# A four-layer graph network on one core: moving a product's scaling from VectorE to ScalarE and GpSimd in the first layer

## The chip, the cores and the metric

The program runs on one core of a Trainium2 chip. The metric is the device time of one execution in microseconds (us). Beside it stands the profile of one execution: its span is the time between the first and the last instruction that the profiler recorded. TensorE is PE in the profile (PEld is its weight load), VectorE is DVE, ScalarE is ACT, GpSimd is POOL and SyncE is SP.

## The reference, cut to what matters

Sixteen inputs `x` of 512 nodes by 128 features pass through four layers, each followed by a residual sum and a layer norm. The change is in the first layer alone, and in one step of the preparation of the second:

```python
def _conv(x, adj):
    return x * jnp.sum(adj, axis=1)[None, :, None]
adaptive = softmax(relu(node_vec1 @ node_vec2), axis=1)
outputs = [x]
for adj in (support0, support1, adaptive):     # both supports are adj here
    x1 = _conv(x, adj);  outputs.append(x1)
    x1 = _conv(x1, adj); outputs.append(x1)
out = concatenate(outputs, axis=2) @ W + b
x = _layernorm(x + out)
...
A_hat = A_norm * dinv[:, None] * dinv[None, :]  # second layer, dinv = rsqrt(deg)
```

`_conv` only scales a node's row by a number. So the layer is a sum of five products of `x` with 128x128 weights, `x @ (W0+I) + s*(x @ Wa) + s^2*(x @ Wb) + a*(x @ Wc) + a^2*(x @ Wd) + b`, with `s` and `a` one number for each node (`coef[:, 0..3, t]`).

## The kernel before

The first stage (`phase_a`) treats the sixteen inputs in eight pairs, and software-pipelines three things over ten slots: slot q has the first layer of pair q (`now`), the aggregation with the 512x512 `A_hat` for pair q-1 (`one`) and the hidden product of pair q-2 (`two`). Each engine has its own instruction queue, written out by hand in `slot(q, ...)`, and executes it strictly in order; semaphores tie the queues together.

A pair has four node tiles t = 0..3 of 128 nodes (both inputs of the pair side by side, so 128x256 elements). For each tile:

- TensorE, `products(q, t)`: the five products into three PSUM banks; even and odd tiles have banks of their own, so `products(q, t)` waits until tile t-2 has been mixed (`mixed`). `products(q, 0)` also waits for the high and low parts of `x` (`xt_hi`, `xt_lo`).
- ScalarE, `scale_first(q, t)` (L467): `mix = coef0 * product 1`.
- VectorE, `combine(q, t)`: three chained multiply-adds (L658), one for each of products 2, 3 and 4, then the plain product 0 (L660).
- GpSimd, `add_bias(q, t)` (L324): adds the bias row. After it VectorE takes the statistics (`count_mix`, L673); after tile 3 they become `rstd` (GpSimd computes the power, L110) and `shift` (L683, `shift_of`).
- In the next slot ScalarE normalizes (`norm`, L478), rounds to the high part (`split_x1`, L486), GpSimd subtracts for the low part (`split_x1`, L329), and TensorE aggregates (L141 to L143, `psum<-shared`).

The order of the queues in a slot of the middle (q = 2 to 6) is, with the other input's work written as i = 0, 1:

- GpSimd: bias of tile 0, `split_x1` 0, bias of tile 1, `split_x1` 1 (L329), bias of tile 2, `split_x` 0 of the next pair (L318), bias of tile 3, `split_x` 1 (L318), the power (L110).
- ScalarE: `scale_first` 0, `norm` 0 (needs `shift`), `scale_first` 1, `split_x1` 0, `keep_z` 0 (L497), `norm` 1, `scale_first` 2, `keep_z` 1, `split_x1` 1, `scale_first` 3, `split_x` (L428), two pieces of later layers' weights (L508), `split_agg` 0 and 1 (L491).
- VectorE: `combine` 0, `combine` 1, `count_z` 0 (L666), `combine` 2, statistics of tiles 0 and 1, `combine` 3, statistics of tile 2, `low_agg` 0 (L678), statistics of tile 3, the moments (L117 to L122, L714), `count_z` 1, `low_agg` 1, two pieces of weights (L689), `shift_of`.

Slot 0 also prepares `A_hat`: `ask_dinv`, the power on GpSimd, then `spread_dinv` (L635) writes `dinv` on the diagonals of four 128x128 tiles, which TensorE spreads over the partitions and GpSimd squares. In slot 1 GpSimd also has the four low parts of `A_hat` (L337). In slot 7 no next pair is split.

Of the kernel before, what the change touches and what calls it, by code (L numbers as in the profile page):

```python
# [8 lines left out]
ALU = mybir.AluOpType  # L9
# [22 lines left out]
def need(eng, sem, value):  # L32

    if isinstance(value, int) and value <= 0:
        return
    eng.wait_ge(sem, value)
# [109 lines left out]
def first_half(nc, sem, psum, banks, ident, exponent, scale2, shift2, x_t, adj_n, adj_t, nv1_t, nv2, l0_w, l0_b,  # L146
# [6 lines left out]
    with ExitStack() as ctx:  # L153
# [64 lines left out]
        agg_done, agg_hi, agg_lo = sem("agg_done"), sem("agg_hi"), sem("agg_lo")  # L218
        z_done, z_kept, z_counted = sem("z_done"), sem("z_kept"), sem("z_counted")
        bn1_ready = sem("bn1_ready")  # L220
        r_ready = sem("r_ready")
        o2_done, o2_kept, o2_counted, o2_stored = sem("o2_done"), sem("o2_kept"), sem("o2_counted"), [sem("o2_stored0"), sem("o2_stored1")]

        k_alpha, rates_ready, cols_ready, k_bc, rates_spread, an_ready, at_ready = (
# [14 lines left out]
        def kept_in(q):  # L239

            return range(2 * (q - 2), 2 * (q - 1)) if 2 <= q < PAIRED else range(0)

        def scaled_block(t, k):

            first = 3 * (t % 2)
            if k < 2:
                return psum[:, first + 2, :].rearrange("p (i k d) -> p i k d", i=2, k=2)[:, :, k, :]
            return psum[:, first:first + 2, (k - 2) * D:(k - 1) * D]
# [60 lines left out]
        @block.gpsimd  # L309
        def _(pool):  # L310
            roots = Roots(asked, rooted, exponent)
            nc.gpsimd.memset(exponent[:], -0.5).then_inc(exponent_ready, 1)
            pool.wait_ge(exponent_ready, 1)

            def split_x(q, i):

                pool.wait_ge(xt_hi, 2 * q + i + 1)
                nc.gpsimd.tensor_tensor(xtl[:, i, :], xt[:, i, :], f32(xth[:, i, :]), ALU.subtract).then_inc(xt_lo, 1)  # L318

            def add_bias(q, t):  # L320

                pool.wait_ge(mixed, NT * q + t + 1)
                m = mix[:, q % 2, :, t, :]
                nc.gpsimd.tensor_tensor(m, m, bias_rows[:], ALU.add).then_inc(biased, 1)  # L324

            def split_x1(q, i):

                pool.wait_ge(x1_hi, 2 * q + i + 1)
                nc.gpsimd.tensor_tensor(x1l[:, i, :, :], x1[:, i, :, :], f32(x1h[:, i, :, :]), ALU.subtract).then_inc(x1_lo, 1)  # L329

            def square_dinv():
                pool.wait_ge(dinv_spread, 1)
                nc.gpsimd.tensor_tensor(squares, diag, diag, ALU.mult).then_inc(dinv_squared, 1)

            def low_ahat(t):
                pool.wait_ge(ahat_hi, t + 1)
                nc.gpsimd.tensor_tensor(ahat_l[:, t, :], ahat[:, t, :], f32(ahat_h[:, t, :]), ALU.subtract).then_inc(ahat_lo, 1)  # L337

            def low_w1():
                pool.wait_ge(w1_hi, 1)  # L340
                nc.gpsimd.tensor_tensor(w1l[:], w1raw, f32(w1h[:]), ALU.subtract).then_inc(w1_lo, 1)

            def slot(q, now, more, one, two):
                if q == 1:
                    low_ahat(0)
                    low_ahat(1)
                for t in range(2):
                    if now:
                        add_bias(q, t)
                    if q == 1:  # L350
                        low_ahat(2 + t)
                    if one:
                        split_x1(q - 1, t)
                if q == 0:
                    roots.answer(nc, pool, dinv[:])
                if now:
                    add_bias(q, 2)
                if more:
                    split_x(q + 1, 0)
                if q == 0:  # L360
                    square_dinv()
                if now:
                    add_bias(q, 3)
                if more:
                    split_x(q + 1, 1)
                if q == 1:
                    low_w1()
                if now:
                    roots.answer(nc, pool, rstd[:])
                if q == PAIRED:  # L370
                    nc.gpsimd.tensor_tensor(gate_bias[:], bihs[:], bhhs[:], ALU.add)

            for i in range(2):
                split_x(0, i)
            pool.wait_ge(c_adjt, 16)
            for t in range(NT):
                ins = nc.gpsimd.tensor_tensor(diag[:, t, :], tile(adjt[:, t, :], t), ident[:], ALU.mult)
            ins.then_inc(diag_ready, 1)
            pool.wait_ge(bias_ready, 1)
            phase_a(slot)  # L380

            def spread_diagonal(v, column):
                for t in range(NT):
                    ins = nc.gpsimd.tensor_scalar(diags[v][:, t, :], ident[:], column[:, t:t + 1], None, ALU.mult)
                ins.then_inc(cols_ready, 1)

            def less_identity():
                pool.wait_ge(c_an, 16)
                pool.wait_ge(kept_lo, len(KEPT))
                for t in range(NT):  # L390
                    nc.gpsimd.tensor_tensor(tile(at[:, t, :], t), tile(at[:, t, :], t), ident[:], ALU.subtract)
                    ins = nc.gpsimd.tensor_tensor(tile(an[:, t, :], t), tile(an[:, t, :], t), ident[:], ALU.subtract)
                ins.then_inc(an_ready, 1)
                pool.wait_ge(an_ready, 1)

            def scale_t(t):
                pool.wait_ge(rates_spread, 1)
                nc.gpsimd.tensor_tensor(at[:, t, :], at[:, t, :], rates_bc, ALU.mult).then_inc(at_ready, 1)

            def low_t(t):  # L400
                pool.wait_ge(at_hi, t + 1)
                nc.gpsimd.tensor_tensor(at_l[:, t, :], at[:, t, :], f32(at_h[:, t, :]), ALU.subtract)

            pool.wait_ge(x1_ready, B)
            spread_diagonal(0, row_sums)
            roots.answer(nc, pool, sc1[:])
            pool.wait_ge(k_alpha, 1)
            nc.gpsimd.tensor_scalar(rates[:], small["alphas"][:], DT * 0.5, None, ALU.mult).then_inc(rates_ready, 1)
            pool.wait_ge(rates_ready, 1)
            spread_diagonal(1, rates)  # L410
            less_identity()
            for t in range(NT):
                scale_t(t)
            for t in range(NT):
                low_t(t)
            roots.answer(nc, pool, scale2[:])

        @block.scalar
        def _(act):
# [44 lines left out]

            def scale_first(q, t):
                act.wait_ge(prod_done, NT * q + t + 1)
                nc.scalar.activation(mix[:, q % 2, :, t, :], scaled_block(t, 1), ACT.Identity,  # L467
                                     scale=coef[:, 0, t:t + 1]).then_inc(scaled, 1)

            def norm(q, i, tiles):  # L470
                if 0 in tiles:
# [38 lines left out]
            def slot(q, now, more, one, two):  # L510
# [26 lines left out]
                    split_x1(q - 1, 1)  # L537
                if now:
                    scale_first(q, 3)
                if more:  # L540
                    for i in range(2):
                        split_x(q + 1, i)
# [48 lines left out]
        def _(dve):  # L591
# [21 lines left out]
            logits_max(3)  # L613
            chain.link(nc.vector.reduce_sum(coef[:, 0, 2:4], adjn[:, 2:4, :], AX_X))
            nc.vector.tensor_copy(row_sums[:], coef[:, 0, :])
            nc.vector.tensor_tensor(coef[:, 1, :], coef[:, 0, :], coef[:, 0, :], ALU.mult)
            dve.wait_ge(exp_ready, NT)
            chain.link(nc.vector.reciprocal(smax[:, 3, :], smax[:, 2, :]))
            chain.link(nc.vector.tensor_tensor(coef[:, 2, :], smax[:, 2, :], smax[:, 3, :], ALU.mult))
# [2 lines left out]
            def ask_dinv():  # L622
# [4 lines left out]
                chain.link(nc.vector.tensor_tensor(deg[:, 2, :], coef[:, 0, :], deg[:, 0, :], ALU.add))  # L627
                chain.link(nc.vector.tensor_tensor(deg[:, 3, :], deg[:, 2, :], deg[:, 1, :], ALU.subtract))
                nc.vector.tensor_scalar(dinv[:], deg[:, 3, :], 1.0, None, ALU.add).then_inc(asked, 1)

            def spread_dinv():

                dve.wait_ge(rooted, 1)
                for t in range(NT):
                    ins = nc.vector.tensor_scalar(diag[:, t, :], ident[:], dinv[:, t:t + 1], None, ALU.mult)  # L635
                ins.then_inc(dinv_spread, 1)

            def scale_ahat():

# [13 lines left out]
            def combine(q, t):  # L653

                m = mix[:, q % 2, :, t, :]
                dve.wait_ge(scaled, NT * q + t + 1)
                for k in (2, 3, 4):
                    chain.link(nc.vector.scalar_tensor_tensor(out=m, in0=scaled_block(t, k), scalar=coef[:, k - 1, t:t + 1],  # L658
                                                              in1=m, op0=ALU.mult, op1=ALU.add))
                nc.vector.tensor_tensor(m, m, scaled_block(t, 0), ALU.add).then_inc(mixed, 1)  # L660
# [7 lines left out]

            def count_mix(q, tiles):
                for t in tiles:  # L670
                    dve.wait_ge(biased, NT * q + t + 1)
                    for i in range(2):
                        ins = nc.vector.bn_stats(stats[:, NT * i + t, :], mix[:, q % 2, i, t, :])  # L673
                return ins
# [16 lines left out]
            def slot(q, now, more, one, two):  # L691
# [6 lines left out]
                    count_z(q - 2, 0)  # L698
                if now:
                    combine(q, 2)  # L700
                if q == 0:
                    spread_dinv()
                if now:
                    count_mix(q, (0, 1))
                    combine(q, 3)
# [1420 lines left out]
```

## Time and profile before

| | us |
|---|---|
| median of 3 runs (lowest, highest) | 946.24 (945.43, 946.3) |
| the profiled execution | 944.95 |
| its span | 943.2 |
| first `scale_first` of the first stage starts | 17.17 |
| last `shift` of the first stage (slot 7) | 149.43 |
| second half of the program begins | 202.4 |
| distance from one `shift` to the next, slots 2 to 6 | 15.97 to 15.99 |
| TensorE, VectorE, ScalarE, GpSimd busy over the span | 899.0, 657.0, 575.6, 320.4 |

The first stage is the stretch from 17 to 150 us. The lines of the timeline name start, duration, engine, source line, operation, written and read buffers, shape, how many of its kind stand together, and in square brackets the idle time of the engine just before it with what ended it.

### The profile page before, as it was taken

The page shows a single profiled execution, that of the slowest core. Times are in us where ns is not written, and L with a number is a line of the kernel's source. Part 1 is how long each engine was busy: PE and PEld are TensorE (multiplying, and loading weights), DVE is VectorE, ACT ScalarE, POOL GpSimd, SP SyncE. Part 2 cuts the span into 40 slices and gives each one's busy share as a digit, 9 for nine tenths or more (in the row PEclk, how much of TensorE's full clock was granted, in tenths as well). Part 3 has the DMA queues.
Part 4 walks back from the last instruction along what each step waited for, and adds up shares of the span by engine and source line. Part 5 has one row for each costly group of instructions (what it writes and reads, how often), then busy time and mean ns, then how long its engine had stood idle before and what let it go on. Part 6 is the DMA issues. An engine that isn't in the chain of part 4 may idle for free.

```text
span 943.2 us, 14724 instructions
## 1 busy us (share of the span) xinstructions
PE 899.0 (95%) x5051; PEld 779.9 (83%) x5051; DVE 657.0 (70%) x1592; ACT 575.6 (61%) x1292; POOL 320.4 (34%) x527
## 2 busy tenths in 40 slices
PE   8799999989998899999999999999999999999996
PEld 6688887457787688989998998999899899978986
DVE  5889996675577675577667758676775866675644
ACT  5457675853555665468657846865784686476352
POOL 2665653530210532144136214423621442340121
PEclk9999999999999999999999999999999999999998
DMA  5222211211101000101201010120101001000000
GB/s 184 101 90 68 68 46 45 100 68 56 34 1 57 8 27 12 46 12 35 68 1 45 18 52 1 45 67 1 38 20 57 2 23 46 1 12 24 11 23 23
DMA packets 26596, 38.56 MB, mean 41 GB/s; under 512 B 3333, under 2 KB 12422, under 8 KB 26010
## 3 DMA queue, kind: packets, MB, share of 16 engines
q1 hardware_dynamic: 26088, 36.05, 11.5%
q10 hardware_dynamic: 434, 1.57, 0.5%
q8 instruction: 40, 0.66, 0.3%
q14 instruction: 34, 0.28, 0.1%
HBM read 21.89 MB, written 15.73 MB: 40 GB/s over the span
## 4 chain that ended last, share of the span: by engine, by line
PE 67%; DVE 7%; ACT 3%; issue 1%; POOL 1%; ACTq 0%; POOLq 0%; DVEq 0%
PE psum L141 18%; PE psum L143 18%; PE psum L142 18%; PE psum L1822 3%; PE psum L1823 3%; PE psum L1826 3%; PE psum L1862 1%; ACT gate L1378 1%; PE psum L1969 1%; PE psum L1838 1%; DVE in_h L1543 1%; PE psum L1883 1%; ACT gate L1381 0%; DVE in_l L1547 0%; DVE e L1755 0%
## 5 line engine op out<-in xcount | busy, mean ns | idle before, releaser
L1378 ACT ACTIVATE gate<-psum,gate_bias 128x256 f32<-128x256 f32 (+2 forms) x296 | 144.0, 560 | 65.2 <-PE psum L1826 54.9
L141 PE MATMUL psum<-in_h,wih_h 128*128 128x256 f32 (+2 forms) x312 | 107.3, 344 | 11.2 <-DVE in_l L1547 7.9
L143 PE MATMUL psum<-in_h,wih_l 128*128 128x256 f32 (+2 forms) x312 | 104.6, 335 | 0.0
L142 PE MATMUL psum<-in_l,wih_h 128*128 128x256 f32 (+2 forms) x312 | 104.2, 334 | 0.0
L141 PEld LDWEIGHTS psum<-in_h,wih_h 128*128 128x128 f32 x312 | 59.3, 190 | 21.3 <-DVE in_l L1547 9.6
L1528 DVE TENSOR_TENSOR gate<-gate 128x256 f32<-128x256 f32 (+2 forms) x48 | 24.2, 503 | 71.9 <-ACT gate L1378 71.0
L1345 POOL TENSOR_TENSOR gate<-in_h,in_l 128x512 f32<-128x512 f32 x14 | 18.0, 1308 | 160.8 <-DVE in_l L1547 160.8
L1381 ACT ACTIVATE gate<-cell 128x512 f32<-128x512 f32 (+2 forms) x80 | 40.3, 503 | 47.1 <-DVE cell L1531 36.4
L142 PEld LDWEIGHTS psum<-in_l,wih_h 128*128 128x128 f32 x312 | 59.7, 191 | 5.3 <-issue 0.2
L143 PEld LDWEIGHTS psum<-in_h,wih_l 128*128 128x128 f32 x312 | 59.8, 192 | 4.8
L141 PE MATMUL psum<-e_h,shared 128*128 128x384 f32 x180 | 61.4, 341 | 1.6 <-DVE gl L1630 1.6
L143 PE MATMUL psum<-e_h,shared 128*128 128x384 f32 x180 | 60.6, 336 | 0.0
L142 PE MATMUL psum<-e_l,shared 128*128 128x384 f32 x180 | 60.5, 336 | 0.0
L141 PE MATMUL psum<-shared 128*128 128x512 f32 x140 | 56.5, 404 | 2.1 <-POOL shared L329 1.2
L1822 PE MATMUL psum<-st_h,whh_h 128*128 128x256 f32 (+2 forms) x192 | 57.3, 316 | 0.4 <-DVE st_h L1536 0.4
L1823 PE MATMUL psum<-st_h,whh_l 128*128 128x256 f32 (+2 forms) x192 | 57.0, 315 | 0.0
L143 PE MATMUL psum<-shared 128*128 128x512 f32 x140 | 54.8, 391 | 0.0
L142 PE MATMUL psum<-shared 128*128 128x512 f32 x140 | 54.6, 390 | 0.0
L1338 POOL TENSOR_TENSOR shared<-raw,shared 128x512 fp32r<-128x512 f32 x14 | 18.8, 1344 | 102.7 <-ACT shared L1446 102.7
L658 DVE SCALAR_TENSOR_TENSOR mix<-psum,coef,mix 128x256 f32<-128x256 f32 x96 | 46.2, 482 | 9.3 <-ACT mix L467 7.0
L1303 POOL TENSOR_TENSOR x_mv<-x_stats 128x4 f32<-128x4 f32 x28 | 9.6, 343 | 118.8 <-DVE x_stats L1553 118.8
L141 PE MATMUL psum<-wmix_h,shared 128*128 128x384 f32 (+1 forms) x128 | 41.4, 324 | 8.3 <-DVE mix L660 5.8
(395 smaller groups left out, 2908.5 us busy)
## 6 DMA issues: line engine op xcount, KB each, us to landing
x_spill<-x SPq DMA_DIRECT2D x30, 256.0 KB, 2.0
xt<-in_x_t_dram SPq DMA_DIRECT2D x16, 256.0 KB, 2.7
raw<-x_spill SPq DMA_DIRECT2D x16, 256.0 KB, 2.9
o_spill<-xt SPq DMA_DIRECT2D x14, 256.0 KB, 2.0
xt<-o_spill SPq DMA_DIRECT2D x14, 256.0 KB, 3.4
x<-x_spill SPq DMA_DIRECT2D x14, 256.0 KB, 3.6
out_dram<-raw SPq DMA_DIRECT2D x14, 256.0 KB, 2.3
raw<-in_adj_t_dram ACTq DMA_DIRECT2D x1, 1024.0 KB, 8.8
```

Of the source, the lines that this page charges most:

```text
L141: pe.matmul(dst, lh, rh, start=start, stop=False, **kw)
L142: pe.matmul(dst, lh, rl, start=False, stop=False, **kw)
L143: return pe.matmul(dst, ll, rh, start=False, stop=stop, **kw)
L658: chain.link(nc.vector.scalar_tensor_tensor(out=m, in0=scaled_block(t, k), scalar=coef[:, k - 1, t:t + 1], in1=m, op0=ALU.mult, op1=ALU.add))
L1338: nc.gpsimd.tensor_tensor(low[:], x3[:, j, :, :], f32(high[:]), ALU.subtract).then_inc(x3_lo, 1)
L1345: nc.gpsimd.tensor_tensor(whole_state(g, j).rearrange("p (w c) -> p c w", c=4), f32(mod4(in2_h)[:, :, j, :]), f32(mod4(in2_l)[:, :, j, :]) ...
L1378: nc.scalar.activation(gate[q][:, 0:n], banks[GATE_BANK[q]][:, 0:n], ACT.Tanh if q == 2 else ACT.Sigmoid, bias=gate_bias[:, p - 1, q:q + 1 ...
L1381: nc.scalar.activation(gate[2][:, 0:n], cell[:, 0:n], ACT.Tanh).then_inc(tanh_ready, 1)
L1528: nc.vector.tensor_tensor(gate[0][:, 0:n], gate[0][:, 0:n], gate[2][:, 0:n], ALU.mult)
L1822: pe.matmul(bank, tile(whh_h[:, p - 2, :], q), st_h[:, 0:n], start=False, stop=False)
L1823: pe.matmul(bank, tile(whh_l[:, p - 2, :], q), st_h[:, 0:n], start=False, stop=False)
L1826: pe.matmul(banks[GATE_BANK[q]][:, 0:n], tile(whh_h[:, p - 2, :], q), st_l[:, 0:n], start=False, stop=True).then_inc(gate_sum, 1)
```

## The change

In the first layer ScalarE now makes two scaled products for each tile: besides product 1 into `mix` it writes product 2, scaled by the squared row sum, into a side buffer `side(t)` (half of `conv_bias`, which the first half of the program does not otherwise use; two tiles share it in turn). VectorE's `combine` has two multiply-adds in place of three. GpSimd first adds the bias row to the side buffer, and then, when VectorE is done with the tile, the side buffer to `mix`; it has two additions for each tile in place of one. ScalarE waits for the side buffer of tile t-2 to be used up. `spread_dinv` moves from VectorE's queue (behind `combine(0, 2)`) to ScalarE's (behind `scale_first(0, 3)`).

```diff
-            def add_bias(q, t):
-
+            def add_side(q, t):
+
+                pool.wait_ge(scaled, NT * q + t + 1)
+                nc.gpsimd.tensor_tensor(side(t), side(t), bias_rows[:], ALU.add).then_inc(biased, 1)
                 pool.wait_ge(mixed, NT * q + t + 1)
+                pool.wait_ge(biased, 2 * (NT * q + t) + 1)
                 m = mix[:, q % 2, :, t, :]
-                nc.gpsimd.tensor_tensor(m, m, bias_rows[:], ALU.add).then_inc(biased, 1)
+                nc.gpsimd.tensor_tensor(m, m, side(t), ALU.add).then_inc(biased, 1)
...
             def scale_first(q, t):
                 act.wait_ge(prod_done, NT * q + t + 1)
+                need(act, biased, 2 * (NT * q + t - 1))
+                if q == 0 and t == 0:
+                    act.wait_ge(squares_ready, 1)
+                nc.scalar.activation(side(t), scaled_block(t, 2), ACT.Identity, scale=coef[:, 1, t:t + 1])
                 nc.scalar.activation(mix[:, q % 2, :, t, :], scaled_block(t, 1), ACT.Identity,
                                      scale=coef[:, 0, t:t + 1]).then_inc(scaled, 1)
+
+            def spread_dinv():
+
+                act.wait_ge(rooted, 1)
+                for t in range(NT):
+                    ins = nc.scalar.activation(diag[:, t, :], ident[:], ACT.Identity, scale=dinv[:, t:t + 1])
+                ins.then_inc(dinv_spread, 1)
...
                 dve.wait_ge(scaled, NT * q + t + 1)
-                for k in (2, 3, 4):
+                for k in (3, 4):
...
-                    dve.wait_ge(biased, NT * q + t + 1)
+                    dve.wait_ge(biased, 2 * (NT * q + t + 1))
```

`add_bias(q, t)` is called `add_side(q, t)` at the same four places of GpSimd's queue, and VectorE's `spread_dinv` (the same four products with `tensor_scalar`) is removed.

## Rows read from the trace of the kernel before

**Rows 1.** Windows over slot 3: length, busy us (instructions) by engine, granted clock

```profile
70.19:86.18 15.99, 15.54 (x87) 13.69 (x86) 15.05 (x41) 11.07 (x24) 9.58 (x9) 1.00 0.21 68
```

**Rows 2.** Timeline of TensorE, slot 1 and slot 3: its longest waits there

```profile
38.23 0.45 PE L141 MATMUL psum<-wmix_h,shared 128*128 128x384 f32 x1 [2.59 <-DVE mix L660]
...
72.30 0.44 PE L141 MATMUL psum<-wmix_h,shared 128*128 128x384 f32 x1 [0.45 <-DVE mix L660]
```

**Rows 3.** Timeline of VectorE, slot 3

```profile
70.19 0.16 DVE L683 SCALAR_TENSOR_TENSOR shift<-mv,rstd 128x8 f32<-128x8 f32 x1
70.27 1.52 DVE L658 SCALAR_TENSOR_TENSOR mix<-psum,coef,mix 128x256 f32<-128x256 f32 x3
...
80.86 0.69 DVE L678 TENSOR_TENSOR aggl<-psum,aggh 128x512 fp32r<-128x512 f32 x1
81.47 0.47 DVE L673 BATCH_NORM_STATS2 stats<-mix 128x6 f32<-128x128 f32 x2
...
86.18 0.16 DVE L683 SCALAR_TENSOR_TENSOR shift<-mv,rstd 128x8 f32<-128x8 f32 x1
```

**Rows 4.** Timeline of ScalarE, slot 3

```profile
70.39 1.65 ACT L478 ACTIVATE x<-mix,shift,rstd 128x128 f32<-128x128 f32 x4 [1.18 <-DVE shift L683]
71.95 0.45 ACT L467 ACTIVATE mix<-psum,coef 128x256 f32<-128x256 f32 x1
...
75.32 0.47 ACT L467 ACTIVATE mix<-psum,coef 128x256 f32<-128x256 f32 x1
75.68 1.06 ACT L497 COPY z<-psum 128x512 f32<-128x512 f32 x2
76.62 0.64 ACT L486 CAST shared<-x 128x512 fp32r<-128x512 f32 x1
77.52 0.47 ACT L467 ACTIVATE mix<-psum,coef 128x256 f32<-128x256 f32 x1 [0.25 <-PE psum L143]
...
80.24 0.59 ACT L491 CAST aggh<-psum 128x512 fp32r<-128x512 f32 x1 [0.18 <-PE psum L143]
```

**Rows 5.** Timeline of GpSimd, slot 3

```profile
77.34 1.29 POOL L329 TENSOR_TENSOR shared<-x,shared 128x512 fp32r<-128x512 f32 x1 [2.10 <-ACT shared L486]
78.59 0.74 POOL L324 TENSOR_TENSOR mix<-mix,rows_bc 128x256 f32<-128x256 f32 x1
79.28 1.29 POOL L318 TENSOR_TENSOR shared<-xt,shared 128x512 fp32r<-128x512 f32 x1
80.54 0.74 POOL L324 TENSOR_TENSOR mix<-mix,rows_bc 128x256 f32<-128x256 f32 x1
```

**Rows 6.** Timeline of GpSimd, end of the first stage: an instruction behind a wait on its own engine

```profile
166.22 0.23 POOL L408 TENSOR_SCALAR rates<-alphas 128x4 f32<-128x4 f32 x1
166.55 2.34 POOL L384 TENSOR_SCALAR mix<-ident,rates 128x128 f32<-128x128 f32 x4
```

**Rows 7.** Timeline of GpSimd, slot 1: first and last of 12 rows without idle time

```profile
38.28 2.54 POOL L337 TENSOR_TENSOR shared<-z,shared 128x512 fp32r<-128x512 f32 x2 [4.02 <-ACT shared L502]
...
51.04 0.74 POOL L341 TENSOR_TENSOR w1l<-z,w1h 128x256 fp32r<-128x256 f32 x1
```

**Rows 8.** Timeline of VectorE, slots 0, 1 and 7

```profile
24.68 2.42 DVE L635 TENSOR_SCALAR z<-ident,dinv 128x128 f32<-128x128 f32 x4
...
30.59 0.49 DVE L673 BATCH_NORM_STATS2 stats<-mix 128x6 f32<-128x128 f32 x2 [0.45 <-POOL mix L324]
...
49.96 0.49 DVE L673 BATCH_NORM_STATS2 stats<-mix 128x6 f32<-128x128 f32 x2 [0.93 <-POOL mix L324]
...
134.12 0.16 DVE L683 SCALAR_TENSOR_TENSOR shift<-mv,rstd 128x8 f32<-128x8 f32 x1
...
145.39 0.48 DVE L673 BATCH_NORM_STATS2 stats<-mix 128x6 f32<-128x128 f32 x2
```

**Rows 9.** Timeline of ScalarE: after the last `shift`, and where the second half begins

```profile
149.62 1.65 ACT L478 ACTIVATE x<-mix,shift,rstd 128x128 f32<-128x128 f32 x4 [2.15 <-DVE shift L683]
...
202.44 0.81 ACT L1417 ACTIVATE xt<-xt,shift,scale 128x512 f32<-128x512 f32 x1 [5.92 <-PEq L153]
```

More of the change, by code:

```diff
@@ L220, in first_half @@
         bn1_ready = sem("bn1_ready")
-        r_ready = sem("r_ready")
+        r_ready, squares_ready = sem("r_ready"), sem("squares_ready")
         o2_done, o2_kept, o2_counted, o2_stored = sem("o2_done"), sem("o2_kept"), sem("o2_counted"), [sem("o2_stored0"), sem("o2_stored1")]
@@ L241, in kept_in, with side @@
             return range(2 * (q - 2), 2 * (q - 1)) if 2 <= q < PAIRED else range(0)
+        def side(t):
+            return conv_bias[:, 2 * (t % 2):2 * (t % 2) + 2, :]
         def scaled_block(t, k):
@@ L348, in slot @@
                     if now:
-                        add_bias(q, t)
+                        add_side(q, t)
                     if q == 1:
@@ L356, in slot @@
                 if now:
-                    add_bias(q, 2)
+                    add_side(q, 2)
                 if more:
@@ L362, in slot @@
                 if now:
-                    add_bias(q, 3)
+                    add_side(q, 3)
                 if more:
@@ L539, in slot @@
                     scale_first(q, 3)
+                if q == 0:
+                    spread_dinv()
                 if more:
@@ L615, in _ @@
             nc.vector.tensor_copy(row_sums[:], coef[:, 0, :])
-            nc.vector.tensor_tensor(coef[:, 1, :], coef[:, 0, :], coef[:, 0, :], ALU.mult)
+            nc.vector.tensor_tensor(coef[:, 1, :], coef[:, 0, :], coef[:, 0, :], ALU.mult).then_inc(squares_ready, 1)
             dve.wait_ge(exp_ready, NT)
@@ L629, in ask_dinv @@
                 nc.vector.tensor_scalar(dinv[:], deg[:, 3, :], 1.0, None, ALU.add).then_inc(asked, 1)
[L631 to L636, printed above, removed]
             def scale_ahat():
@@ L700, in slot @@
                     combine(q, 2)
-                if q == 0:
-                    spread_dinv()
                 if now:
```

## The prediction

> **What bounds the kernel now.** The change touches only the first stage, so I read first the windows over its slots, then the timeline of each engine in a middle slot, slot 3, and then the slots that differ (0, 1 and 7). The windows show an engine pair near its limit: in 15.99 us TensorE is busy for 15.54 and VectorE for 15.05, ScalarE for 11.07 and GpSimd for 9.58, with the full clock (2.4 GHz) granted [rows 1]. By shares alone the change looks right: it takes work from a full engine and gives it to two that have 5 and 6 us free. But an in-order queue can be late with half its time free, so what counts is the closed chains that run from one `shift` to the next. There are two of almost the same length.
>
> *Chain A, through VectorE and TensorE.* TensorE's only wait in slot 3 is for tile 0's mix, 0.45 us before `products(q, 2)` [rows 2]. The mix comes from `combine(q, 0)`, which starts at once behind `shift` [rows 3]. From there TensorE runs without a gap until the aggregation's first half is done; ScalarE rounds it at 80.24, after a wait of 0.18 for TensorE [rows 4], VectorE takes it at 80.86 and is busy without a gap until the next `shift` at 86.18 [rows 3]. This chain sets today's period, 86.18 - 70.19 = 15.99 us.
>
> *Chain B, through ScalarE and GpSimd.* Behind `shift`, ScalarE normalizes at 70.39, and in its queue order comes to `split_x1` of the second input at 76.62 [rows 4]. GpSimd has idled 2.10 us for it and starts its low part at 77.34; then bias of tile 2, low part of x, bias of tile 3, each on the heels of the other, the last from 80.54 to 81.28 [rows 5]. VectorE takes the statistics of tile 3 at 81.47 [rows 3]; with some 0.03 us for the hand-over it could have done so at 81.31. Chain B is thus 0.16 us short of binding: its length is 15.83 us (7.15 from `shift` to GpSimd's start, 3.94 in GpSimd's queue, 0.03, and 4.71 from 81.47 to 86.18).
>
> **The change part by part.**
>
> *VectorE's multiply-add.* Three take 1.52 us, so one is 0.51 [rows 3]; four fewer in a slot are 2.0 us. On chain A only the one of tile 0 counts: A shrinks from 15.99 to 15.48. On chain B there is no `combine` at all, so B gains nothing.
>
> *ScalarE's second scaling.* It has the shape of L467, whose follower starts 0.36 us after it (75.32 to 75.68) [rows 4]. Four of them go in a slot. Two of the four (tiles 1 and 2) stand in the queue between `norm` and `split_x1` of the second input, a stretch in which ScalarE has no idle time: B grows by 0.72. The lower bound is this 0.36, the upper the whole duration of 0.47 [rows 4], that is 0.94 for two.
>
> *GpSimd's second addition.* Same shape and operands as L324, 0.74 us [rows 5]. The second addition waits on a semaphore of the first; where GpSimd waited for its own previous instruction, 0.10 us lay between (166.45 to 166.55) [rows 6]. So each tile costs 0.84 more. Queued behind `split_x1` of the second input are both additions of tile 2 and both of tile 3; the side addition can't be done in the 2.10 us of idle time ahead, because the order of the queue puts it behind the low part. B grows by 2 x 0.84 = 1.68. Lower bound 0.70 apiece (78.59 to 79.28 is 0.69, without a wait), upper 0.94, with the gap taken twice. The Trainium skill's page "GPSIMD Engine Reference", section "Engine selection", speaks against the move: elementwise additions with two inputs belong on VectorE, being about half as fast here. Its ratio changes no term above, since the row has a duration for the same addition.
>
> *The period.* B becomes 15.83 + 0.72 + 1.68 = 18.23 us. It passes A, so slots 2 to 6 go from 15.99 (15.98 on average) to 18.23: 2.25 each, five of them, **+11.2 us**. Bounds: 15.83 + 0.72 + 1.40 - 15.98 = 1.97 and 15.83 + 0.94 + 1.88 - 15.98 = 2.67 each. What is late next: GpSimd's last low part of x (behind tile 3's additions) releases `products` 0 of the next pair, so TensorE's idle time in a slot rises by the same 2.25 and moves to the head of the slot. The side buffer's wait is free: both additions of tile t-2 end over 1 us before ScalarE comes to tile t in these slots, by the same queue order.
>
> *Slot 1.* GpSimd works from 38.28 to 51.78 without a gap, since it has the four low parts of `A_hat` too [rows 7], and VectorE waits 0.93 us for its bias of tile 3 [rows 8]. Here every addition lengthens the queue: all four side additions stand before that wait, 4 x 0.84 = **+3.4 us** (2.8 to 3.8). ScalarE will wait here for the side buffer (tile 3 for tile 1), some 3 us, but it idled later in this slot anyway, and GpSimd doesn't wait for it.
>
> *Slot 7.* There is no next pair, and VectorE takes tile 3 at 145.39, 11.27 us behind `shift` at 134.12 [rows 8]. By the new queue: 7.15 + 0.72 to GpSimd's start, 1.25 for the low part (77.34 to 78.59), 0.84 + 0.69 for tile 2, 0.84 + 0.74 for tile 3, 0.03: 12.26. **+1.0 us** (0.7 to 1.4).
>
> *Slot 0, with `spread_dinv`.* VectorE loses 2.42 us of it between tile 2 and its statistics [rows 8], ScalarE gains four copies of 128x128 (some 0.39 each by L478: 70.39 to 71.95 is 1.56 for four [rows 4]), in a part of the slot where it otherwise waits for TensorE. VectorE then waits for GpSimd's tile 3 anyway, as it does now for 0.45 us [rows 8]; GpSimd's queue gains three or four side additions but starts each tile earlier. I work out about 0.3 us earlier for `shift`, and as much later for `norm` in slot 1, which stands behind one more scaling of tile 1: **0** (-1 to +1). Its cover is that wait of GpSimd; without it it would be worth up to 2.4 us.
>
> *What follows the stage.* ScalarE waits 2.15 us for the last `shift` [rows 9]; the rest of the first half (aggregation, batch statistics of all inputs) hangs on it, and the second half starts for all engines together at 202.44, where ScalarE had idled 5.92 us for TensorE's queue [rows 9]. Nothing absorbs the delay.
>
> Sum: 11.2 + 3.4 + 1.0 + 0 = 15.6 us. The profiled execution took 944.95, so 960.6; the median of the runs is 1.3 us above it, 946.24 + 15.6 = **961.8 us**, +1.65%. Bounds: 5 x 1.97 + 2.8 + 0.7 - 1 = 12.4 and 5 x 2.67 + 3.8 + 1.4 + 1 = 19.6, so 958.6 to 965.8 as its own range.
>
> **The rivals.**
>
> *Chain A goes on deciding (faster).* If the additions cost chain B under 0.16 us a slot, the period becomes A's, 15.48: six slots (2 to 7) x 0.5 = 3.0 us less, 943.2. For it: VectorE's 15.05 of 15.99 [rows 1], and TensorE's wait for the mix [rows 2]. Against it: 2.4 us would have to vanish from a queue that shows no gap [rows 5]. The point from which it decides is that 0.16. The Trainium skill would lean this way: "Perfetto Trace Analysis", section "Optimizing Scalar/DVE Operations", says that with a saturated VectorE moving work to ScalarE or even GpSimd may make sense, though not surely between VectorE and GpSimd. Chance 0.04.
>
> *Only ScalarE's part counts.* If GpSimd's additions hid, ScalarE's three scalings ahead of `split_agg` would be 1.08, less the waits of 0.25 and 0.18 that they fill [rows 4]: about +0.6 a slot, 3 to 5 us in all with slot 1, 949 to 951. Against it: same queue as above. Chance 0.04. No measurable change would need a mix of this with the first: 0.02.
>
> *TensorE's clock.* If the longer idle stretch at each slot's head cost the clock, `products` 0 and 1 (3.5 us) would run at 1.2 GHz and take twice as long; ScalarE's tile 1 then comes about 1.8 us late, which lies on chain B: 5 x 1.8 = +9, 971. Against it: a wait of 2.59 us in slot 1 left the next matmuls at 0.45 us and less [rows 2]. The skill's page "TensorE: Matmul & The Clock Gate", section "HAM oscillation", warns of such a fall with idle gaps; the new gap of 2 to 3 us would be of the size that this trace bears. Additions on GpSimd slower than the rows have them are another way past 968. Chance of the two together: 0.06.
>
> **How the numbers follow.** My forecast has 0.84. The range is 955 to 968: it adds to the own range of 958.6 to 965.8 a part for slot 0 and slot 1, where I placed the queues less surely, and leaves out the rivals. Within 0.2% (1.9 us) a measurement of this kernel can't tell a change from none. Faster 0.04, same 0.02, slower 0.94.
>
> **What would show it.** Right: `shift` to `shift` is about 18.2 us in slots 2 to 6; L658 64 times, L467 and its neighbour 32 each, 64 additions of 0.74; in each slot VectorE idles about 1.5 us before the statistics of tile 3, released by GpSimd; TensorE idles over 2 us before `products` 0, released by L318; GpSimd goes without idle time from L329 to the second L318. Wrong: if the statistics of tile 3 wait for nothing, or the period is under 17 us. My sum fails most easily in the wait of GpSimd on itself, which enters 16 times, and in slot 1.

## The result, and the profile after

| | before | after |
|---|---|---|
| median (lowest, highest), us | 946.27 (945.43, 946.44) | 968.35 (967.23, 969.64) |
| the profiled execution, its span | 944.95, 943.2 | 969.64, 967.5 |
| first scaling of the first stage to the start of the second half | 185.27 | 207.02 |
| `shift` to `shift`, slots 3 to 6 | 15.98 | 18.96 to 18.98 |

The ratio is 1.025 (95% interval 1.0225 to 1.0275): 22.1 us slower, where 15.6 were forecast. The first stage alone, up to the start of the second half, is 21.75 us longer in the profiled execution, so the loss lies in the stage that the change touches. (The spans differ by 2.5 us more. The second half of these two executions is 744.5 against 740.8 us long, with the same work: TensorE is busy for 715.2 against 711.5 us on the same 4200 matmuls, and near 869 us its granted clock is 0.50 where the kernel before has 1.00 at the same place. The second half varies as much between other runs, from 739.2 us in `scalar_only` to 744.1 in `count_first`, so it is not part of what the change costs.)

Three parts of the stage carry it, each from the starts of `shift` in the timeline of VectorE:

| part | before | after | difference | forecast |
|---|---|---|---|---|
| first scaling to `shift` of slot 1 | 37.03 | 41.75 | +4.7 | +3.4 |
| five periods, slots 2 to 6 | 79.92 | 95.31 | +15.4 | +11.2 |
| slot 7 | 15.31 | 16.99 | +1.7 | +1.0 |
| last `shift` to the second half | 53.01 | 52.97 | 0 | 0 |

The page's first lines say that the work did move, off VectorE (657 us before) and onto ScalarE (575.6) and GpSimd (320.4). TensorE has the same matmuls and is busy 11 us longer, 8 in the first stage and 3.7 in the second half; stretches at a lower clock, shown further down, are in both:

```profile
PE 910.2 (94%) x5051; PEld 787.4 (81%) x5051; DVE 642.0 (66%) x1556; ACT 587.7 (61%) x1328; POOL 342.9 (35%) x559
```

The window of slot 4 answers to [rows 1] (length, then busy us of TensorE, its weight load, VectorE, ScalarE and GpSimd, granted clock, DMA share, GB/s). No engine is near its limit any longer: an order of waits sets the period, not a full engine.

```profile
96.13:115.09 18.96, 16.22 (x86) 13.76 (x86) 13.85 (x37) 12.30 (x28) 12.98 (x14) 1.00 0.18 56
```

Timeline of GpSimd in the same slot, the answer to [rows 5] (L336 is the old L329, L322 the old L318, L327 the side addition, L331 the addition to `mix`):

```profile
95.54 1.27 POOL L327 TENSOR_TENSOR conv_bias<-conv_bias,rows_bc 128x256 f32<-128x256 f32 x1 [0.59 <-ACT mix L478]
...
104.53 1.30 POOL L336 TENSOR_TENSOR shared<-x,shared 128x512 fp32r<-128x512 f32 x1 [1.86 <-ACT shared L504]
105.79 0.74 POOL L327 TENSOR_TENSOR conv_bias<-conv_bias,rows_bc 128x256 f32<-128x256 f32 x1
106.67 0.73 POOL L331 TENSOR_TENSOR mix<-mix,conv_bias 128x256 f32<-128x256 f32 x1
107.37 1.29 POOL L322 TENSOR_TENSOR shared<-xt,shared 128x512 fp32r<-128x512 f32 x1
108.62 0.74 POOL L327 TENSOR_TENSOR conv_bias<-conv_bias,rows_bc 128x256 f32<-128x256 f32 x1
109.50 0.73 POOL L331 TENSOR_TENSOR mix<-mix,conv_bias 128x256 f32<-128x256 f32 x1
110.19 1.26 POOL L322 TENSOR_TENSOR shared<-xt,shared 128x512 fp32r<-128x512 f32 x1
```

And VectorE's, the answer to [rows 3]:

```profile
94.93 1.28 DVE L702 TENSOR_TENSOR adj_l<-raw,adj_h 128x512 fp32r<-128x512 f32 x2
96.13 0.70 DVE L696 SCALAR_TENSOR_TENSOR shift<-mv,rstd 128x8 f32<-128x8 f32 x1
...
110.33 0.49 DVE L686 BATCH_NORM_STATS2 stats<-mix 128x6 f32<-128x128 f32 x2 [1.81 <-POOL mix L331]
110.85 0.62 DVE L117 TENSOR_TENSOR mv<-stats 128x8 f32<-128x8 f32 x1
```

The reader is to see three things. The queue of GpSimd behind 104.53 is closed up, as forecast, and VectorE waits 1.81 us for its last addition. The addition to `mix` starts 0.88 us after the side addition, not 0.84. And two VectorE instructions on 128x8 elements, whose neighbours of the same shape take 0.16 to 0.17, take 0.62 and 0.70: each ends when the GpSimd instruction beside it ends. L117 ends at 111.47, L322 at 111.45; `shift` ends at 96.83, the side addition at 96.81, itself stretched from 0.74 to 1.27 because it started beside VectorE's two subtractions L702. A wait for another engine stands here as a duration, not in square brackets. The first period that begins with such a `shift` is that of slot 3: the one at the head of slot 2 (57.72) takes 0.17, because tile 0's side addition only starts at 58.61 there.

The first of the two was in the kernel before as well, where I had passed over it. Timelines of VectorE and of GpSimd in slot 3 of before:

```profile
81.98 0.58 DVE L117 TENSOR_TENSOR mv<-stats 128x8 f32<-128x8 f32 x1
```

```profile
81.23 1.30 POOL L318 TENSOR_TENSOR shared<-xt,shared 128x512 fp32r<-128x512 f32 x1
```

Both end at 82.53 to 82.56. So chain B of the kernel before ran to the end of GpSimd's *next* instruction, the second low part of x: 7.15 to GpSimd's start, 3.89 to 81.23, 1.30, 0.03, and 3.62 from 82.56 to `shift`: 15.99 us. It was not 0.16 short of binding; it bound. After, by the same steps: 8.40 (7.15 + 0.72 for ScalarE + 0.54 for the stretched `shift`), 5.66, 1.26, 0.02, 3.62: 18.96.

In the Trainium skill, "SBUF — State Buffer", section "SBUF: two separate sides", has the rule: VectorE with two SBUF inputs and GpSimd share a pair of ports under an exclusive lock; who starts first has it for the whole instruction, and the other stands still. The two traces agree: L117 (two inputs in SBUF) stands for 0.4 us behind L318, and `shift` for 0.54 behind the side addition.

Slot 1 shows something else. Timeline of TensorE, then the window over its first 6 us:

```profile
30.14 0.41 PE L141 MATMUL psum<-wmix_h,shared 128*128 128x384 f32 x1 [2.29 <-issue]
...
32.22 0.52 PE L141 MATMUL psum<-wmix_h,shared 128*128 128x384 f32 x1
```

```profile
30.00:36.00 6.00, 5.72 (x26) 5.54 (x27) 5.38 (x16) 1.36 (x4) 1.69 (x2) 0.72 0.17 49
```

Behind an idle stretch of 2.29 us the matmuls of 128x384 first keep their 0.34, then go to 0.52 from 32.22 on (the 1.2 GHz level), and are back at 0.34 by 36. The kernel before has in the same place (its idle stretch there is 1.72 us):

```profile
31.70:37.70 6.00, 3.77 (x24) 3.59 (x24) 5.53 (x16) 2.49 (x7) 1.74 (x2) 1.00 0.17 48
```

### The profile page after: what moved, and what is told of

Read it like the earlier page. It is cut to its first block, busy times and chain, and to the rows that moved or that the text cites. A ratio compares the mean times of both kernels' runs of the same rounds, so it can differ in the third digit from the quotient of the medians.

```text
span 967.5 us, 14819 instructions
## 1 busy us (share of the span) xinstructions
PE 910.2 (94%) x5051; PEld 787.4 (81%) x5051; DVE 642.0 (66%) x1556; ACT 587.7 (61%) x1328; POOL 342.9 (35%) x559
## 4 chain that ended last, share of the span: by engine, by line
PE 66%; DVE 7%; ACT 3%; issue 1%; POOL 1%; ACTq 0%; POOLq 0%; DVEq 0%
PE psum L141 18%; PE psum L143 18%; PE psum L142 18%; PE psum L1834 3%; PE psum L1833 3%; PE psum L1837 3%; PE psum L1873 1%; ACT gate L1389 1%; PE psum L1980 1%; PE psum L1849 1%; DVE in_h L1554 1%; PE psum L1894 1%; ACT gate L1392 0%; DVE in_l L1558 0%; DVE e L1766 0%
## 5 line engine op out<-in xcount | busy, mean ns | idle before, releaser
L141 PE MATMUL psum<-in_h,wih_h 128*128 128x256 f32 (+2 forms) x312 | 108.2, 347 | 11.2 <-DVE in_l L1558 7.9
L141 PE MATMUL psum<-shared 128*128 128x512 f32 x140 | 57.7, 412 | 4.5 <-POOL shared L336 3.4
L143 PE MATMUL psum<-shared 128*128 128x512 f32 x140 | 55.6, 397 | 0.0
L142 PE MATMUL psum<-shared 128*128 128x512 f32 x140 | 55.3, 395 | 0.0
L141 PE MATMUL psum<-adj_h,node_h 128*128 128x512 f32 x120 | 47.5, 396 | 1.9 <-POOL node_l L1340 1.2
```

The costliest lines, as they stand in the source:

```text
L141: pe.matmul(dst, lh, rh, start=start, stop=False, **kw)
L142: pe.matmul(dst, lh, rl, start=False, stop=False, **kw)
L143: return pe.matmul(dst, ll, rh, start=False, stop=stop, **kw)
```

## The experiments

All changes of length given for the stage run from the first scaling to the start of the second half, in the profiled execution: 185.27 before, 207.02 after.

**The two parts by themselves.** `scalar_only`: `side` is written by ScalarE and never read, all else as before. `gpsimd_only`: `side` is zeroed once, GpSimd adds the bias row to it and then the bias row to `mix`; ScalarE and VectorE as before.

The cuts show the instruction that each adds; the waits and the zeroing around it are left out.

```diff
 scalar_only: before plus
+                nc.scalar.activation(side(t), scaled_block(t, 2), ACT.Identity, scale=coef[:, 1, t:t + 1])
 gpsimd_only: before plus
+                nc.gpsimd.tensor_tensor(side(t), side(t), bias_rows[:], ALU.add).then_inc(biased, 1)
```

> The kernel before, with ScalarE's second scaling added (into the side buffer, which nobody reads; VectorE keeps its three multiply-adds, so the output is complete). The queue theory (the period is the longer of two chains, and two of the four scalings lie on the chain through ScalarE and GpSimd, 15.83 us long before): 15.83 + 0.72 = 16.55 us from shift to shift against 15.98, so about +0.6 in each of slots 2 to 6 and 7, +3.2 us in all, 949.5. The rival that ScalarE's free time hides it (ScalarE is busy for 11 of 16 us): 946.3, period 15.98.

> The kernel before, with GpSimd's second addition added at the place where the change has it (on a zeroed side buffer that nobody reads; bias, ScalarE and VectorE as before, output complete). Queue theory alone: 15.83 + 2 x 0.88 = 17.6 us a slot, with slots 1 and 7 about +13 us, 959. With the port theory (GpSimd's addition of tile 0 runs beside VectorE's two-input subtractions and shift, and all of them stand still for about 0.54 us, on both chains) 18.1 us a slot and shift lasts 0.70 in place of 0.16: about +16, 962. Rival: the free time of GpSimd hides it, 946.3. Second rival, the excess over the forecast comes from TensorE's clock: shift stays at 0.16.

`scalar_only` ran in 952.19 against 944.55, ratio 1.008 (1.0048 to 1.0111); period 16.70, stage +4.96. 15.99 + 0.72 is 16.71: the forecast's 0.72 was exact, and nothing of it vanished in a slack. `gpsimd_only` ran in 962.69, ratio 1.0199 (1.0174 to 1.0223); period 18.24, stage +15.6. Its timelines of GpSimd and VectorE show the collision of tile 0's side addition on the subtractions instead of `shift`:

```profile
110.36 1.03 POOL L328 TENSOR_TENSOR conv_bias<-conv_bias,rows_bc 128x256 f32<-128x256 f32 x1 [0.22 <-ACT mix L475]
```

```profile
110.11 1.82 DVE L697 TENSOR_TENSOR wih_l<-adjn,wih_h 128x512 fp32r<-128x512 f32 x2
111.86 0.15 DVE L691 SCALAR_TENSOR_TENSOR shift<-mv,rstd 128x8 f32<-128x8 f32 x1
```

1.82 in place of 1.28, `shift` 0.15: again 0.54, whoever is the one to stand. The two periods add up: 15.98 + 0.72 + 2.26 = 18.96. So the period has 0.72 of ScalarE, 1.76 of two longer pairs of additions in the queue, and about 0.5 of the collision.

**Two positions of a side addition.** `early_side2` puts tile 2's side addition into GpSimd's idle time ahead of the low part of the second input (in slot 0, where there is none, behind the power). `late_side0` makes tile 0's wait until VectorE has mixed the tile, which is after `shift`.

```diff
 early_side2
+                    if t == 1 and now and q > 0:
+                        side_first(q, 2)
                     if one:
                         split_x1(q - 1, t)
...
 late_side0
-                pool.wait_ge(scaled, NT * q + t + 1)
+                pool.wait_ge(mixed if t == 0 else scaled, NT * q + t + 1)
                 nc.gpsimd.tensor_tensor(side(t), side(t), bias_rows[:], ALU.add).then_inc(biased, 1)
```

> The changed kernel with one edit of the order in GpSimd's queue: the side addition of tile 2 goes ahead of the second low part, into the 1.86 us for which GpSimd idles there. Same instructions. Queue theory: the period of 18.97 loses one addition with its gap, 0.87, in slots 2 to 6 and in slot 7: -5.2 us, 963.1. If only busy time or the memory port counted, nothing would change: 968.3.

> The changed kernel, where GpSimd's side addition of tile 0 waits for VectorE's mix of tile 0, so that it no longer runs beside VectorE's two subtractions of weights and shift. Port theory: L327 of tile 0 takes 0.74 in place of 1.27, shift 0.16 in place of 0.70, period 18.97 - 0.54 = 18.43, six slots: -3.2 us, 965.1. Rival (shift is long for a reason of its own, or the excess is the clock): no change, 968.3. The added wait itself costs nothing, GpSimd idles 0.81 us behind tile 0.

`early_side2`: 962.48, ratio 1.0195 (1.017 to 1.0219), period 18.12, 0.85 less, one addition and its gap. `late_side0`: 966.46, ratio 1.0246 (1.0216 to 1.0276), period 18.42, 0.55 less, and `shift` short again:

```profile
114.32 0.16 DVE L696 SCALAR_TENSOR_TENSOR shift<-mv,rstd 128x8 f32<-128x8 f32 x1
```

The addition still costs GpSimd its 0.74; it only stands elsewhere. This is the run that shows the collision as the cause of the 0.54, since no work left the kernel. (Slot 2 has no collision at its head in either run, and gains nothing: 19.73 against 19.43.)

**Does VectorE's relief help anywhere?** `tile0_only`: the change for tile 0 alone, slots 2 to 7, where by the forecast it shortens chain A and not chain B. `reorder_only`: ScalarE does `split_x1` of the second input ahead of `keep_z`, to relieve chain B. `tile0_and_reorder` has both.

```diff
 tile0_only
+        def relieved(q, t):
+
+            return t == 0 and q >= 2
...
-                for k in (2, 3, 4):
+                for k in ((3, 4) if relieved(q, t) else (2, 3, 4)):
 reorder_only
-                if two:
-                    keep_z(q - 2, 1)
                 if one and now:
                     split_x1(q - 1, 1)
+                if two:
+                    keep_z(q - 2, 1)
```

> The kernel before, with the change's relief for tile 0 alone and only in slots 2 to 7: ScalarE scales product 2 of tile 0 into the side buffer, VectorE has two multiply-adds there, and GpSimd does both additions of tile 0 behind VectorE's mix (so not beside VectorE's subtractions). All other tiles as before. Queue theory: none of this lies on the chain through ScalarE and GpSimd (15.83 us); the chain through VectorE and TensorE drops from 15.98 to 15.47, so the first one decides: period 15.83 to 15.85, -0.15 in six slots, -0.9 us, no measurable difference (945.4 for a before of 946.3). Rival (VectorE's work is what bounds the stage): -0.5 a slot, -3 us. Rival (GpSimd's additions cost wherever they stand): +0.8 a slot, +5 us.

> The kernel before, with one swap in ScalarE's queue in every slot: the second input's rounding (split_x1 1) goes ahead of the copies of the hidden product (keep_z 1). Queue theory: the chain through ScalarE and GpSimd drops by 0.94 to 14.9 us, but the other one (15.98) decides, so the period and the time stay as they are (within 0.2%).

> Both edits together. Queue theory: now both chains are shorter, 15.47 and 14.9 us, and the period becomes 15.47: -0.5 us in six slots, -3.0 us, ratio 0.997, although each edit alone gives nothing or 0.9 us. If the theory of two nearly equal chains is wrong, the sum of the two single edits.

Ratios 1.0001 (0.9984 to 1.0019), 1.0014 (0.9997 to 1.0031), 1.0008 (0.9988 to 1.0027); periods 15.99, 15.98, 15.98. For the first I had expected a period of 15.83 to 15.85, for the last 15.47 and 3 us; both failed, since they still stood on the slack of 0.16 in chain B. In `tile0_only` L117 takes 0.66 and ends with GpSimd's last low part, so chain B alone explains it. In `tile0_and_reorder` L117 still takes 0.38, and another wait has come up: the aggregation starts 7.20 us behind `shift` (6.98 in `tile0_only`), behind the `keep_z` that was moved back, and VectorE waits 0.21 us for its rounding. The period is the meeting point of several chains of nearly one length; shortening two of them by a step each gave nothing.

**Taking the port wait away.** `count_first`: VectorE takes the statistics of `z` (L666, one input in SBUF) between tile 3's statistics and the moments, so that L117 comes after GpSimd's low part instead of standing beside it. `dinv_only`: before, with only `spread_dinv` moved to ScalarE.

```diff
 count_first
-                    chain.link(count_mix(q, (NT - 1,)))
+                    counted = count_mix(q, (NT - 1,))
+                    if two:
+                        counted.then_inc(dve1, 1)
+                        chain.n += 1
+                        count_z(q - 2, 1)
+                        dve.wait_ge(dve1, chain.base + chain.n)
...
                     moments(nc, chain, stats, mv, 2 * NT)
...
```

> The kernel before, where VectorE takes the statistics of the hidden product (count_z 1, one input each) ahead of the moments (L117 and on, two SBUF inputs) and not behind them. New theory from the traces: in the kernel before, too, L117 doesn't take its 0.17 but 0.58 us, because it ends only when GpSimd's last low part of x ends (82.53 and 82.56); so the chain through GpSimd ran to that end, and was 15.99 us long, not 15.83. With this swap L117 meets no GpSimd work: 0.17, and both chains lose about 0.4 us: period 15.6, six slots, -2.3 us, ratio 0.9975. If L117 is long for a reason of its own, it stays at 0.58 and the period at 15.98 or above.

> The kernel before, with spread_dinv moved from VectorE to ScalarE and nothing else. My forecast had 0 for it. Worked out anew from the changed kernel's trace: VectorE's tile 3 of slot 0 is mixed 2.3 us earlier, GpSimd's bias and last low part of x follow, so shift of slot 0 comes 1 to 2.3 us earlier and products of slot 1 start 1 to 2 us earlier. If TensorE keeps its full clock there, -1 to -2 us in all, 944.5 to 945.3; if the clock theory holds (granted clock 0.72 in that stretch of the changed kernel), slot 1's first two products take over 5 us in place of 3.7 and the gain is gone, 946.3.

`count_first`: 943.93 against 946.02, ratio 0.9978 (0.9962 to 0.9994), period 15.50, stage -2.1. Its timeline of VectorE, with the same work in another order:

```profile
95.24 1.27 DVE L666 BATCH_NORM_STATS2 zstats<-z 128x6 f32<-128x512 f32 x2
96.43 0.15 DVE L117 TENSOR_TENSOR mv<-stats 128x8 f32<-128x8 f32 x1
```

GpSimd's low part ran from 94.60 to 95.89 beside L666, which kept its length (1.28 before). What the swap takes away is the port wait of 0.4 us in each slot. TensorE now has no idle time in a period at all, as the window over slot 4 says, so its own work is what bounds this version:

```profile
83.54:99.06 15.52, 15.52 (x86) 13.70 (x85) 14.60 (x42) 11.06 (x24) 9.58 (x9) 1.00 0.21 68
```

`dinv_only` shortens its stage by 1.6 us in the profile: `shift` of slot 0 comes 2.0 us earlier behind the first scaling (16.32 for 18.32), and slot 1 gives back 0.4. Its time doesn't resolve that (1.0, 0.9982 to 1.0018).

**All that might help.** `all_but_tiles_1_to_3` puts together `tile0_and_reorder`, `count_first`, `dinv_only` and `keep_z` of the first input ahead of `split_x1`. The cut shows this last edit alone.

```diff
+                if two and now:
+                    keep_z(q - 2, 0)
                 if one:
                     split_x1(q - 1, 0)
-                if two:
+                if two and not now:
                     keep_z(q - 2, 0)
```

> A version meant to beat both: relief of tile 0 alone behind VectorE's mix, spread_dinv on ScalarE, statistics of the hidden product ahead of the moments, and in ScalarE's queue keep_z 0 ahead of split_x1 0 and split_x1 1 ahead of keep_z 1. By the chains: the one through VectorE 15.98 - 0.51 - 0.4 = 15.1, the one through GpSimd 15.99 - 0.94 - 0.4 = 14.65, the one over keep_z 0 and TensorE 15.77 - 0.36 - 0.4 = 15.0; TensorE's own work of 15.3 us then decides. Period 15.3 to 15.5, -0.5 to -0.7 in six slots, and -1.6 for spread_dinv: -4.6 to -5.6 us, ratio 0.995. If GpSimd's port or the order costs elsewhere, the period stays above 15.7 and the ratio above 0.997.

941.4, ratio 0.9958 (0.9943 to 0.9973), stage -2.86, but period 15.66: longer than `count_first` alone, because TensorE waits 0.15 us in each slot for the `keep_z` of the second input (L522), which was moved back. I left the relief of tile 0 and the two moves out again.

**TensorE's clock in slot 1.** `after_filled` is after with twice as many filler matmuls in slot 0, ahead of the idle stretch.

```diff
-                    keep_busy(8, 6)
+                    keep_busy(16, 6)
```

> The changed kernel with eight more filler matmuls at the end of slot 0 (16 in place of 8), in the 2.29 us in which TensorE waits for GpSimd. Clock theory: the products of tiles 0 and 1 of slot 1 took 5.3 us there at a granted clock of 0.72 of 2.4 GHz, against 3.8 before; with the gap filled they take 3.8 and the first stage is 1.5 us shorter: 966.8. Rival (the clock is drawn by chance and not by the gap): no change in the mean, 968.3.

965.1, ratio 1.0194 (1.0164 to 1.0224), stage 207.02 to 204.39. TensorE idles 0.49 us in place of 2.29 ahead of the same matmul, and the clock stays:

```profile
30.00:36.00 6.00, 4.28 (x27) 4.10 (x28) 5.82 (x17) 3.02 (x8) 1.66 (x1) 1.00 0.17 49
```

The fall itself is no accident of one execution: `early_side2`, `late_side0` and `after_three_repairs` idle 2.28 to 2.29 us at this place too, and all three have 0.50 from 32 to 34 us. Of the 2.6 us, 1.5 come up to the `shift` of slot 1 and 1.15 in slots 2 and 3. In the changed kernel the clock was low again later in slot 1, and its last fall reaches into slot 2; with the fillers the same window has the full clock. The changed kernel, then `after_filled`:

```profile
52.00:58.00 6.00, 3.64 (x16) 3.26 (x15) 3.07 (x11) 0.89 (x2) 4.88 (x5) 0.80 0.33 87
```

```profile
52.00:58.00 6.00, 4.87 (x30) 4.68 (x31) 4.28 (x14) 2.56 (x7) 4.45 (x5) 1.00 0.21 66
```

This last fall isn't explained by the length of the idle stretch ahead of it: TensorE idles 2.36 us there in the changed kernel and 2.63 in `after_filled`, which keeps its clock. So 0.67 us of the 1.15 (slot 2, 19.43 to 18.76) go with the clock of that stretch, but why the fillers spared it is open. The other 0.48 are no clock: at 74.84 the `shift` of `after_filled` takes 0.16, because tile 0's side addition starts only at 74.82, behind the subtractions. Without the collision slot 3 takes 18.50 in place of 18.98.

**The sum turned round.** `after_three_repairs` is after with `early_side2`, `late_side0` and `count_first`; `count_first_and_dinv` is before with what survived.

> The changed kernel with three changes of order and no change of its work: side addition of tile 2 ahead of the second low part, side addition of tile 0 behind VectorE's mix, statistics of the hidden product ahead of the moments. If the period is the sum of queue and port terms as measured (18.97 - 0.85 - 0.55 - 0.42), it is 17.15 us, still 1.2 above the period before, because one scaling pair and one addition stay on the chain; the first stage is 10 to 11 us shorter than the changed kernel's: 957.5. If the terms hide one another, the period stays above 17.6 and the time above 960.

> The kernel before with only two edits: statistics of the hidden product ahead of the moments, and spread_dinv on ScalarE. From the traces of the two single edits, first scaling to second half: 185.3 us before, 183.2 and 183.7 with one of them; they act in different slots, so they add up: 181.5, -3.7 us, 942.3 for a before of 946.0, ratio 0.996. The period is 15.5, so the relief of tile 0 adds nothing that this order doesn't give already (the version with all edits had 15.66).

`after_three_repairs`: 956.93, ratio 1.0127 (1.0102 to 1.0151), period 17.03 against the 17.15 expected. Three edits of order, with no work left out, take 1.94 us off a period of 18.97. Not all of it is a repair of the change: 0.85 and 0.55 are, and the rest is the swap that gives the kernel before 0.48 as well. Against `count_first`, which has that swap too, the change still costs 17.03 - 15.50 = 1.53 us a period, about ScalarE's 0.72 and one addition with its gap. `count_first_and_dinv`: 941.8 against 945.96, ratio 0.9962 (0.9943 to 0.9982), period 15.50, stage -3.77, the sum of the two single edits (2.1 and 1.6). It beats both kernels with no `combine` relieved at all: the one useful part of the change was the move of `spread_dinv`, 1.6 to 1.7 us of the stage in the profiles with it against those without.

## Why the prediction was off

The direction, the place and the mechanism were right: ScalarE's and GpSimd's work lies on the path from `shift` to `shift`, VectorE's relief is worth nothing, TensorE's wait moves to the head of the slot (1.75 us before `products` 0, where over 2 were forecast; the 0.45 of [rows 2] is gone), slot 7 and the tail follow. The time was 968.35 where 961.8 was given and 968 was the end of the range. By its steps:

- **"Chain B is thus 0.16 us short of binding."** This failed. I ended GpSimd's part of the chain at the addition that releases the statistics, and took L117's 0.58 in the last stretch as its own time. But L117 stands behind GpSimd's second low part, so that the chain ran to the end of that one. The 0.16 us of slack that I let the change use up didn't exist: 5 x 0.16 = 0.8 us, in `scalar_only` to be read by itself (16.70, not 16.55).
- **The addition of tile 0, costed at nothing.** The change part by part priced only what stands behind `split_x1`. The new addition of tile 0 comes where GpSimd had nothing to do and VectorE has two subtractions with two inputs in SBUF and then `shift`. Its price is 0.54 us ahead of each of slots 3 to 7, so four times in the five periods (2.2 us) and once in slot 7 (0.5), the largest single miss; `late_side0` shows it. It was the cost of *when* an instruction runs, in a stretch that I had called free.
- **GpSimd waiting for itself, 0.10 us [rows 6].** It is 0.14 between the two additions (106.67 - 105.79 - 0.74): 0.88 for each tile, 2 x 0.04 a slot, 0.4 us in all. The bounds held. (In `tile0_only`, where the second addition waits for the first and for nothing else, the gap is 0.08.)
- **ScalarE's 0.36 for each scaling** was right.
- **The period** thus is 15.99 + 0.72 + 1.76 + 0.54 = 19.01, measured 18.97 in slots 3 to 6. Slot 2 has no 0.54 at its head, so 18.43 would be its share, and it took 19.43. Of this 1.0 us, 0.66 lie between `shift` and the second input's low part (57.72 to 66.25 is 8.53, against 7.87 in `after_filled`), where its `products` ran at the lower clock; the other 0.33 are a longer gap between tile 2's two additions (0.48 in place of 0.14), which `after_filled` has at the same place too and whose cause no run here shows.
- **Slots 0 and 1, +3.4.** Slot 0 gave 0.95 us, where I had worked out 0.3 and put 0: the wait for GpSimd that was to cover the move of `spread_dinv` does not cover it, since by itself (`dinv_only`) the move brings that `shift` 2.0 us forward. Slot 1 took 5.7. 1.5 of that is the clock: with the fillers both slots together are 3.2 longer, close to the forecast, though still as the sum of two misses, -0.9 and +4.1. I had weighed the clock only at the head of the middle slots, where no fall is seen with a wait of 1.75 us, and not in slot 1, where TensorE now idles 2.29 us behind its fillers in place of 1.72.
- **Slot 7, +1.0**, was 1.7. 0.54 of the difference is the collision ahead of it, 0.08 the gap between its additions, and the rest some 0.06 in the last addition and its hand-over. L117 takes 0.17 here in both kernels: with no next pair to split, it meets no low part.
- **The rivals** of chain A and of ScalarE alone are out. The one for "additions slower than the rows have them" came nearest, but the additions in the queue are not slower (0.74 and 0.73); only the one of tile 0 is.

Together 0.8 + 2.2 + 0.4 on the periods, 1.0 more for slot 2, 0.7 for slot 7 and 1.3 for slots 0 and 1 are 6.4 us. The stage is 6.15 us longer than forecast (the periods are 0.04 short of their sum), the median 6.55. What stays open: the low clock late in slot 1, the longer gap in slot 2, and why slot 1 without the lower clock at its head still took 4.1 us where 3.4 were forecast.

## What to carry to other kernels

When work goes to GpSimd, look at what VectorE runs at that moment. If that instruction has two inputs in SBUF, one of the two stands still, and the profile books the wait as a longer duration; so compare each duration with the shortest of its shape before calling a chain slack. A queue that is closed up behind a late release takes all that is put into it at full price, however idle its engine is on average; if work must be added, its place should be ahead of that release. And where several chains have almost one length, relief of the fullest engine gives nothing until the others are shorter too.

## What the runs showed of the hardware

- A VectorE instruction of 128x8 elements with two inputs in SBUF, 0.15 to 0.17 us alone, took 0.37 to 0.77 us beside a GpSimd addition or subtraction that was already running, and ended within 0.03 us of it where both ends were read (L117 and `shift`, before and after). One with a single input (L666, 1.27 in `count_first`) or with one of its two inputs in PSUM (L691 at 107.84 in the changed kernel, 0.67 beside L322) was not lengthened.
- Two VectorE subtractions of 128x512 (1.28 us) that meet a GpSimd addition of 128x256 (0.74) bring VectorE's next work 0.54 us later. Either GpSimd shows it (1.27, and then `shift` 0.70) or VectorE (1.82).
- Two dependent GpSimd additions of 128x256 start 0.88 us apart, independent ones 0.69. 0.14 us lies between the end of one and the start of the next, 0.08 in `tile0_only`.
- The granted clock fell some 1.6 us after an idle stretch of 2.29 us had ended, at a time when TensorE was busy again, and stayed at the 1.2 GHz level for some 3.4 us; four traces with 2.28 or 2.29 us show the fall, and the one with 0.49 us doesn't. Waits of 1.75 us in the later slots, between long busy stretches, left it at 1.00.
- The length of an idle stretch doesn't decide it alone. Stretches of 2.59 us (before, 38.23), 2.63 (`gpsimd_only`, 53.65) and 2.63 (`after_filled`, 53.13) left the clock at 1.00, and `tile0_only`, with the idle stretches of before at the same places (1.73 and 2.62 us against 1.72 and 2.59), had 0.50 from 38 to 40 us where before had 1.00.
